# A graph network kernel: edge inputs load first on two queues, the bucket marks are kept for one fused offset pass, the table of tiles moves, and edge tiles are no longer padded to pairs

## The reference, cut to what matters

```python
def _rel_graph_conv_bdd(x, src, dst, etype, norm, w, loop_w, bias):
    xs = x[src].reshape(e, nb, -1)
    we = w[etype]
    msg = jnp.einsum('ebi,ebio->ebo', xs, we)      # 2x2 blocks, one set for each type
    msg = msg.reshape(e, -1) * norm
    agg = jax.ops.segment_sum(msg, dst, num_segments=n)
    return agg + bias + x @ loop_w
```

## Time and profile before

| | |
|---|---|
| timed runs | 7048.02 to 7060.27 us, median 7054.67 (3 runs) |
| profiled execution, its span | 7015.3 us |
| mean granted TensorE clock | 0.903 |
| busy PE | 4991.8 us (71%) |
| busy DVE | 4512.7 us (64%) |
| busy ACT | 2064.0 us (29%) |
| busy POOL | 1454.6 us (21%) |

### The profile page before, as it was taken

One profiled execution on the slowest core, in us unless ns is written; L12 is line 12 of the kernel. 1 busy time (PEld: TensorE's weight loads), 2 busy tenths in 40 slices (PEclk: granted clock), 3 DMA queues, 4 the chain that ended last, 5 costly groups with the idle time before them and its releaser, 6 DMA issues. The chain is left out here.

```text
span 7015.3 us, 73781 instructions
## 1 busy us (share of the span) xinstructions
PE 4991.8 (71%) x21189; PEld 3466.3 (49%) x21189; DVE 4512.7 (64%) x7271; ACT 2064.0 (29%) x3714; POOL 1454.6 (21%) x1466
## 2 busy tenths in 40 slices
PE   0110488888888599989688869579926777667976
PEld 0000244544444466668577648568823333336854
DVE  5994599947999522232398270301049999998867
ACT  0000011122111133322233223222227777763321
POOL 0677666603666100001000010110020000000000
PEclk9999998999999699989899989789968888888978
DMA  1332233454333400014341002256534444433200
GB/s 28 122 132 75 57 112 102 99 188 179 102 114 101 67 9 9 9 46 122 102 137 53 14 25 73 90 163 184 173 93 158 154 155 155 151 107 120 87 13 18
DMA packets 375829, 683.70 MB, mean 97 GB/s; under 512 B 90626, under 2 KB 302651, under 8 KB 367900
## 3 DMA queue, kind: packets, MB, share of 16 engines
q1 hardware_dynamic: 300236, 523.14, 22.7%
q0 software_dynamic: 75344, 157.40, 8.6%
HBM read 507.64 MB, written 172.62 MB: 97 GB/s over the span
## 5 line engine op out<-in xcount | busy, mean ns | idle before, releaser
L812 PE MATMUL ps<-sum_hot_cell,sum_hot_src 128*128 128x500 bf16 x2640 | 771.1, 398 | 323.0 <-DVE sum_hot_src L756 209.2
L734 POOL DMA_INDIRECT sum_rows_in<-rel_table,rel_row x880 | 841.6, 956 | 445.9 <-issue 236.0
L758 DVE TENSOR_SCALAR sum_hot_cell<-x_nodes 128x1500 bf16<-128x1500 f16 (+1 forms) x880 | 892.3, 1014 | 2.3 <-issue 2.3
L1938 PE MATMUL ps<-att_ring,acc 125*65 125x500 f32 x1000 | 602.0, 688 | 307.0 <-DVE att_ring L1759 306.9
L817 PE MATMUL ps<-sum_rows_in,sum_hot 128*128 128x256 f32 x1760 | 596.1, 417 | 56.6 <-issue 52.1
L1876 ACT ACTIVATE att_ring<-att_ring,att_src 125x625 f32<-125x625 f32 x750 | 555.4, 808 | 253.2 <-DVE att_ring L1734 154.2
L1946 PE MATMUL ps<-acc,att_ring 125*125 125x257 f32 x2500 | 557.2, 386 | 42.5 <-DVE att_ring L1759 42.5
L812 PEld LDWEIGHTS ps<-sum_hot_cell,sum_hot_src 128*128 128x128 bf16 x2640 | 268.7, 102 | 614.1 <-issue 420.3
L1946 PEld LDWEIGHTS ps<-acc,att_ring 125*125 125x125 f32 x2500 | 475.8, 191 | 121.1 <-DVE att_ring L1759 46.2
L1700 DVE CUSTOM_DVE_ANT_0 att_masks<-att_masks,aux 125x3125 bf16<-125x3125 bf16 x150 | 510.7, 3411 | 32.3 <-ACT aux L1822 19.2
L1759 DVE SCALAR_TENSOR_TENSOR att_ring<-att_ring,att_cell 125x3125 f32<-125x3125 f32 (+1 forms) x162 | 512.0, 3167 | 1.6 <-ACT att_ring L1876 1.3
(11 more groups left out here) (446 smaller groups left out, 8580.1 us busy)
## 6 DMA issues: line engine op xcount, KB each, us to landing
att_cell<-cells SPq DMA_DIRECT2D x150, 781.2 KB, 4.7
att_masks<-masks SPq DMA_DIRECT2D x150, 762.9 KB
rel_table<-rel_stage SPq DMA_DIRECT2D x50, 2048.0 KB, 6.3
ffn_w<-in_L_ffn_W SPq DMA_DIRECT2D x64, 1024.0 KB, 6.8
sum_cell<-cells SPq DMA_DIRECT2D x125, 156.2 KB, 5.4
sage_cell<-cells SPq DMA_DIRECT2D x125, 156.2 KB, 2.2
masks<-sum_stage POOLq DMA_DIRECT2D x25, 762.9 KB, 12.0
sum_rows_in<-rel_table,rel_row POOLq DMA_INDIRECT x880
```

What stands on the lines that cost most here:

```text
L734: pool.indirect_dma_start(rows_in[:, b, u, :], None, table, bass.IndirectOffsetOnAxis(rows[:, k:k + 1], 0)).then_inc(gathered[b], 16)
L758: dve.tensor_scalar(hot_cell[:, b, u, :], K.columns[:, :, 0:CW], K.cell[:, k], None, ALU.is_equal).then_inc(s_hot, 1)
L812: pe.matmul(K.ps[:, bass.ds(side * 4 + j, 1), 0:BW].rearrange("p a n -> p (a n)"), hot_src[:, b, u, :], hot_cell[:, b, u, j * BW:(j + 1) * ...
L1938: pe.matmul(K.ps[0:W, side, 0:BAND], node_rows[s][0:NPT, h, :], ring[0:NPT, b % RB, v, 0:BAND], start=s == 0, stop=s == NT - 1).then_inc(s ...
```

## The change

1. *Inputs.* `EdgeInput` holds the four edge tiles. DVE fills them at the start of `setup`; SP loads dst and type, ACT loads src and weight, each in 112, 15 and 1 rows. POOL clears the last 32 partitions of x, and x is loaded in the sort phase, behind the default records. DVE waits for dst alone before the buckets, for the rest behind them.
2. *Marks.* `mine` keeps all 25 marks. For each bucket a mark, a scan into PSUM and a `copy_predicated` of the count into `rank`; ACT copies the row totals. The offset pass is one `scalar_tensor_tensor` per bucket. Both loops are written out.
3. *Table of tiles.* Its steps stand at the end of DVE's work in `first_tables`; POOL's iota for it stands ahead of the scatters.
4. *Tiles.* `KT = 420`, `NG = 105`; buckets are padded to one tile. PE loads `tile_of`, holds and computes addresses for every tile.

```diff
-PAIR = 2
-KT = 440
+KT = 420
...
+    def load(self, eng, which):
+        for i in which:
...
+            eng.wait_ge(self.s_filled[i], 1)
+            eng.dma_start(self.tiles[i][0:FULL, :], whole[0:FULL]).then_inc(self.s_loaded[i], 16)
+            eng.dma_start(self.tiles[i][FULL:P - 1, :], whole[FULL:P - 1]).then_inc(self.s_loaded[i], 16)
+            eng.dma_start(self.tiles[i][P - 1:P, 0:TAIL], last).then_inc(self.s_loaded[i], 16)
...
+            pool.wait_ge(iota_done, 2)
+            pool.memset(K.x[96:P, :, :], 0.0).then_inc(K.x_cleared, 1)
...
-            dve.memset(K.x[:, :, :], 0.0).then_inc(zeroed, 1)
+            edges.fill(dve)
...
-            sp.dma_start(K.x[0:112, :, :], x_rows[0:112]).then_inc(loaded, 16)
-            sp.dma_start(K.x[112:NPT, :, :], x_rows[112:NPT]).then_inc(loaded, 16)
-            sp.wait_ge(loaded, 32)
+            edges.load(sp, (0, 2))
+        @block.scalar
+        def _(act):
+            edges.load(act, (1, 3))
...
+            sp.wait_ge(K.x_cleared, 1)
+            sp.dma_start(K.x[0:FULL, :, :], x_rows[0:FULL]).then_inc(K.x_loaded, 16)
+            sp.dma_start(K.x[FULL:NPT, :, :], x_rows[FULL:NPT]).then_inc(K.x_loaded, 16)
             sp.wait_ge(defaults, 16)
+            sp.wait_ge(K.x_loaded, 32)
...
+        @block.scalar
+        def _(act):
+            for t in range(NT):
+                act.wait_ge(s_pick, t + 1)
+                act.copy(rowtot[:, t:t + 1], scan(t)[:, EC - 1:EC]).then_inc(s_total, 1)
...
-            dve.wait_ge(loaded, 8 * 16)
-            link(dve.tensor_copy(dst[:, :], dst_i[:, :]))
+            dve.wait_ge(edges.s_loaded[0], 48)
+            link(dve.tensor_copy(dst[:, :], edges.dst_i[:, :]))
...
+                dve.tensor_scalar(mine[:, t, :], bkt[:, :], bnum[:, t:t + 1], None, ALU.is_equal).then_inc(s_mine, 1)
...
+                if t >= 3:
+                    dve.wait_ge(s_total, t - 2)
+                dve.tensor_tensor_scan(scan(t), one[:, :], mine[:, t, :], 0.0, ALU.mult, ALU.add).then_inc(s_scan, 1)
...
+                dve.copy_predicated(rank[:, :], mine[:, t, :].bitcast(U32), scan(t)).then_inc(s_pick, 1)
...
-            link(dve.tensor_scalar(tiles_i[:, :], ps_tot, float(PAIR * P - 1), None, ALU.add))
-            link(dve.tensor_scalar(tiles_i[:, :], tiles_i[:, :], 8, None, ALU.logical_shift_right))
+            link(dve.tensor_scalar(tiles_i[:, :], ps_tot, float(P - 1), None, ALU.add))
+            link(dve.tensor_scalar(tiles_i[:, :], tiles_i[:, :], 7, None, ALU.logical_shift_right))
...
+            for t in range(NT):
+                if t > 0:
+                    dve.wait_ge(s_rank, t)
+                dve.scalar_tensor_tensor(out=rank[:, :], in0=mine[:, t, :], scalar=offs[:, t:t + 1], in1=rank[:, :],
+                                         op0=ALU.mult, op1=ALU.add).then_inc(s_rank, 1)
...
-            with dve.Fori(0, NT - 1) as b:
-                hold(dve, step, link.n + b)
-                dve.scalar_tensor_tensor(out=dt[:, :], in0=kt[:, :], scalar=ends[:, bass.ds(b, 1)], in1=dt[:, :],
-                                         op0=ALU.is_ge, op1=ALU.add).then_inc(step, 1)
...
+            pool.iota(kt_i[:, :], [[1, KT]], base=0, channel_multiplier=0).then_inc(s_counted, 1)
             for j in range(EC):
...
+            for b in range(NT - 1):
+                dve.wait_ge(s_of, b + 2)
+                dve.scalar_tensor_tensor(out=of_tile[:, :], in0=kt[:, :], scalar=K.ends[:, b:b + 1], in1=of_tile[:, :],
+                                         op0=ALU.is_ge, op1=ALU.add).then_inc(s_of, 1)
...
-                         for k in range(g * G, (g + 1) * G, PAIR)]
+                         for k in range(g * G, (g + 1) * G)]
...
-                for q, tile in enumerate(tiles):
+                for u, tile in enumerate(tiles):
                     side = tile % 2
                     hold(pe, s_free, tile + 1)
-                    for u in range(q * PAIR, q * PAIR + PAIR):
```

More of the change, by code:

```diff
@@ L216, in sort_edges, with scan @@
         block = ph.block()
-        tail = E - (P - 1) * EC
         ps_tot = K.ps[:, 0, 0:NT]
         ps_before = K.ps[:, 1, 0:NT]
+        def scan(t):
+            return K.ps[:, 2 + t % 3, 0:EC]
         @block.sync
         def _(sp):
[L223 to L230, removed]
+            x_rows = K.inp["x"].rearrange("(t p) d -> p t d", p=NPT)
+            sp.wait_ge(defaulted, 2)
@@ L246, in _ @@
-            pe.matmul(ps_before, K.before[:, :], rowtot[:, 0, :], start=True, stop=True).then_inc(sums, 1)
+            pe.wait_ge(s_total, NT)
+            pe.matmul(ps_tot, K.ones[:, :], rowtot[:, :], start=True, stop=True).then_inc(sums, 1)
+            pe.matmul(ps_before, K.before[:, :], rowtot[:, :], start=True, stop=True).then_inc(sums, 1)
         @block.vector
@@ new lines, in pick @@
+            def pick(t):
+                dve.wait_ge(s_scan, t + 1)
+                if t > 0:
+                    dve.wait_ge(s_pick, t)
+                dve.copy_predicated(rank[:, :], mine[:, t, :].bitcast(U32), scan(t)).then_inc(s_pick, 1)
+            mark(0)
+            mark(1)
+            count(0)
+            for t in range(NT):
+                if t + 2 < NT:
+                    mark(t + 2)
+                if t + 1 < NT:
+                    count(t + 1)
+                pick(t)
@@ L275, in _ @@
                                           op0=ALU.mult, op1=ALU.add))
[L276 to L280, removed]
-                          for u in range(UN)])
-                turn.all([dve.tensor_tensor_scan(scan[:, u, :], one[:, :], mine[:, u, :], 0.0, ALU.mult, ALU.add)
-                          for u in range(UN)])
-                turn.all([dve.tensor_copy(rowtot[:, 0, bass.ds(i * UN, UN)], scan[:, :, EC - 1])]
-                         + [dve.tensor_tensor(mine[:, u, :], mine[:, u, :], scan[:, u, :], ALU.mult) for u in range(UN)])
-                for u in range(UN):
-                    turn(dve.tensor_tensor(rank[:, :], rank[:, :], mine[:, u, :], ALU.add))
-                turn.end()
@@ L289, in _ @@
[L289 to L296 removed]
+            link(dve.tensor_copy(rec[:, :, 3], edges.w[:, :]))
@@ L297, in _ @@
+            dve.wait_ge(sums, 2)
+            link(dve.tensor_scalar(tiles_i[:, :], ps_tot, float(P - 1), None, ALU.add))
+            link(dve.tensor_scalar(tiles_i[:, :], tiles_i[:, :], 7, None, ALU.logical_shift_right))
+            link(dve.tensor_copy(tiles[:, :], tiles_i[:, :]))
+            link(dve.tensor_tensor_scan(K.ends[:, :], one[:, 0:NT], tiles[:, :], 0.0, ALU.mult, ALU.add))
+            link(dve.tensor_tensor(offs[:, :], K.ends[:, :], tiles[:, :], ALU.subtract))
             link(dve.tensor_scalar(offs[:, :], offs[:, :], float(P), -1.0, ALU.mult, ALU.add))
@@ L298, in _ @@
             link(dve.tensor_tensor(offs[:, :], offs[:, :], ps_before, ALU.add))
-            with dve.Fori(0, NT // UN) as i:
-                turn = LoopChain(dve, lstep2, i, 2 * UN)
-                turn.all([dve.tensor_scalar(mine[:, u, :], bkt[:, :], bnum[:, bass.ds(i * UN + u, 1)],
-                                            offs[:, bass.ds(i * UN + u, 1)], ALU.is_equal, ALU.mult) for u in range(UN)])
-                for u in range(UN):
-                    turn(dve.tensor_tensor(rank[:, :], rank[:, :], mine[:, u, :], ALU.add))
-                turn.end()
+            dve.wait_ge(s_pick, NT)
```

119 lines of the change are left out of this document (69 added, 50 removed).

## The result

The changed kernel takes 7085.6 us (median of 4 runs, 7064.54 to 7093.94) against 7051.35 for the kernel before (4 runs): ratio 1.0041, interval 1.0024 to 1.0058. It is slower, as forecast, but by some 30 us and not by 180. The time lies in the range that I gave; the size does not.

What follows compares the result with a forecast made beforehand. DVE's sort, POOL's scatters and TensorE in the sums were taken as last, PE's sequencer becoming last in the sums; 7054.7 - 104 (front) + 282 (sums) = 7233 us. The range ran from absorbed stalls (6978, with 13 for the front) to 7420.

Steps and rivals of the forecast that it cites:

- Front: Inputs, sort and table of tiles ahead of and beside the scatters: -104 us, with -83 to -112 as ends.
- the pick: Masked pick of each of 25 buckets in DVE's sort: taken as 0.60 us, between 0.4 and 0.85.
- the fused steps: 25 fused offset steps in DVE's sort, replacing a mark and a sum: 15.3 us (to 22.8) against 30.6.
- The sequencer as the new bound: Edge sums: four loads, holds and address sets make PE's sequencer last, at 6.05 and 6.57 us a group.
- One sign that I had named: PE in the sums: matmuls would stand in clumps of one tile, with gaps put down to issue.
- The rival in which the sequencer runs ahead: Sums: address work overlaps earlier matmuls, pace stays 5.9, 20 fewer tiles save 59 us; 6892 us, chance 0.1.
- multiplied stalls: Sums: stalls fall on the sequencer's doubled instructions, adding 3.1 and 2.3 us a group; 7549 us, chance 0.1.
- the cancelling case: Sums near +104 us cancel the front's gain, leaving the time within 0.2% (14 us); chance 0.05.
- The stalls on top: Sums: today's issue stalls stay above the sequencer's time, 1.35 and 1.1 us a group, giving 7.4 and 7.65.
- the rival with absorbed stalls: Sums: sequencer binds but stalls fall into its time, so sums cost +27 us; 6978 us, chance 0.2.
- The cross-check: Sums: pace in proportion to PE's instructions a group (59 to 77, 65 to 85) gives 7.67 and 7.74, +318 us.
- The rule on fetch: PE's issue in the sums: sequential fetch is hidden, so no stalls and the absorbed rival's time; taken to hold only in part.

Runs made afterwards that it cites:

- e6: The changed kernel run again unchanged, on a chip without the stalls: +41.8 us against the kernel before, ratio 1.0056.
- e4: The kernel before with two more table loads a group whose values go unused: 0 us against the kernel before, ratio 1.0004.
- e13: The kernel before with VectorE and GpSimd doing less in the sums, so TensorE is fed faster: -207.2 us against the kernel before, ratio 0.9693.
- e5: The kernel before run again unchanged, for its own trace beside the experiments: -1 us, ratio 0.9995.
- e1: The changed kernel with tiles padded to pairs again (440 tiles, two loads and holds a group): -110.7 us against the kernel before, ratio 0.9839.
- e12: The changed kernel with its four table loads but one hold a group: -104.8 us against the kernel before, ratio 0.9844.
- e3: The changed kernel with one table load a group filling four registers, holds kept for each tile: -152.4 us against the kernel before, ratio 0.9778.
- e7: The changed kernel with one table load and one hold a group: -164.5 us against the kernel before, ratio 0.9753.

## Why the prediction was right or wrong

**Front: right.** Forecast -104, measured -106 at the first sum's start and -110.7 alone. DVE began at 8.6 and not 12; the 25 buckets took 42.4 us (15.92 to 58.35) and not 48; the pick took 0.58 for my 0.60; the fused steps 16.5 for 15.3. The scatters started at 89.8 for 98.3, 8 us better, and their stage was 11 us longer where I had allowed 3. So two misses of the front cancel; that the sum came out within 2 us is in part luck.

**The sequencer as the new bound: right.** 6.05 and 6.57 us a group, read from the trace of before, stand in the runs without stalls at 6.17 and 6.78. Where it waits for nothing it does exactly that: on the first chip too a group between stalls is 6.06 us (949.28 to 955.34). One sign that I had named came out otherwise: the matmuls stand in clumps of four tiles with one pause, put down to VectorE, and not in clumps of one. A tile's hold and addresses (0.835 us) are shorter than its matmuls (1.07), so TensorE catches up with the sequencer only behind the loads. The rival in which the sequencer runs ahead and the pace stays at 5.9 fell, and so did multiplied stalls: they do hit the sequencer's own instructions, but add nothing like 3.1 and 2.3 us a group. So did the cancelling case, though the time came near it: it needed 104 us from the sums, and they gave 140.

**The stalls on top: the step that failed.** "So I keep them, less the part that is a slow array: 1.35 and 1.1." On the first chip the changed kernel lies 0.71 and 0.36 us a group over the sequencer's 6.05 and 6.57. Over 105 groups that is 67 and 76 us less, the whole of the 142 by which the sums came out shorter than I forecast. And not all of what was measured is stalls: without them (e6) the same kernel lies 0.12 and 0.21 over, so they cost 0.60 and 0.15 us a group, 63 and 16 us (710.3 and 727.8 for e6's 647.7 and 711.7). Of these, 19 and 15 us are the first two groups of the first sum and the first of the second. Outside that one group the second sum shows next to no loss, as the rival with absorbed stalls had it; in the first sum 44 us remain.

The term was mis-sized, and in part from rows that I had. PE's excess over the array has two parts. In one it is idle; in the other it is busy, with slower matmuls, and that part costs nothing once the array has slack. The earlier trace rows give the second: 548.5 us busy, where 440 tiles at 1.07 are 471, so 78 us or 0.70 a group, for which I took off 0.26. In the second sum 576.9 less 440 x 1.18 = 519 leaves 58 us or 0.53, for which I took off 0.1. The other part is the idle time put down to issue, in the rows above 87.5 us (0.80 a group) and 55.0 us (0.50). With these the sums would have been 105 x 6.85 - 646.5 = +73 and 105 x 7.07 - 651.2 = +91, and the forecast 7054.7 - 104 + 164 = 7115, against 7085.6. This removes most of the miss, but with two errors that partly cancel: it leaves out the 0.12 and 0.21 that the kernel has without stalls (35 us), and of the idle part, 0.80 and 0.50, only 0.60 and 0.15 came back (58 us less). Why so little of it is left in the second sum stays open. All of it rests on one trace of each kernel on the first chip, and no experiment met the stalls again.

**The cross-check misled.** That pace in proportion to the number of instructions gave 7.67 and 7.74 (+320 by these figures, and not +318) had no mechanism behind it. Two more loads a group (e4) are six more instructions and cost nothing, on a chip without stalls.

**The rule on fetch.** The Trainium skill (Runtime: NRT & Kernel Launch, Instruction fetch mechanics) says that fetch is hidden, and by it the rival with absorbed stalls would have come out. On the later chips nothing contradicts it: e13 issues at the array's full pace for 440 us with PE busy for 439.04. There too the rival's sums (+27) don't come out, but +157 (647.7 and 711.7 for 589.1 and 612.9), since VectorE's 5.36 and not the stalls' 5.88 is what the new pace is measured against. Whether the stalls of the first chip were fetch is not shown. In the first sum of the kernel before, the queue q8, which carries instructions, has 25 transfers on the first chip and in e5, with medians of 1.02 and 0.97 us. Slower transfers are therefore not seen; late ones aren't excluded.

**What each part is worth.** On the chip of e1 to e12: front -111 (-103 between the two traced executions, 6824.1 and 6927.1), of which the moved table some 7 to 11, uncertain; dropping the pairs +159 with four loads and four holds; -42 on top of the front with one load (e3 against e1); -54 with one load and one hold (e7, 6763.2 us), the fastest that leaves no work out, 164.5 under the kernel before. There VectorE is last in both sums again, and the 20 tiles fewer at last count.

## What to carry to other kernels

An engine's sequencer is an engine too: add up the spacing of its loads, checks, holds and address computations for one turn of a loop, and compare it with the longest data engine before the cover is used up. When a wait is put down to an engine, look whether that engine was itself waiting; if so, the late one is the instruction stream of the waiting engine. When a stall is carried over to a kernel with another bound, split it into idle time and slower work, and take even the idle part as an upper end: here 0.80 and 0.50 us a group became 0.60 and 0.15.

## What the runs showed of the hardware

- A table load that fills four registers takes 333 ns, one that fills one register 298 ns (e3 and the changed kernel). A load with its check costs PE's sequencer 0.65 us, of which the load is 0.35; a hold 0.25 (e3 and e12 against e6).
- The same program took 7051 us in one measurement and 6926 to 6931 on two numbered chips, with a different engine last in the same loop (first measurement and e5). The stalls in which PE waits for nothing on record were in the first measurement only; in one of them single instructions of PE's sequencer took 0.7 us, a load 699 ns for 298.
